# A relational step of TensorE in a graph network on one core: the sums first, then the edge weights, and one drain that carries the only signal

## What is computed

```python
edge_w = edge_attr @ nn_w.T + nn_b
msg = jax.nn.relu(x[src] * edge_w)
out = x @ root + bias
for r in range(N_REL):                      # 3 relations
    m = jnp.where((edge_type == r)[:, None], msg, 0.0)
    s = jax.ops.segment_sum(m, dst, num_segments=n)
    cnt = jax.ops.segment_sum(mask.astype(x.dtype), dst, num_segments=n)
    out = out + (s / jnp.maximum(cnt, 1.0)[:, None]) @ W[r]
```

## Time and profile before

| | |
|---|---|
| runs (us) | 5503.09, 5523.4, 5527.77; median 5523.4 |
| profiled execution (us) | 5528.27, span of its records 5526.4 |
| granted clock of TensorE, mean share of full | 0.81 |
| busy: PE, DVE, POOL, ACT | 68%, 52%, 49%, 27% |
| indirect DMAs of the relational gathers | 1248, 953 ns each on POOL |
| relational stretches, by layer (us) | 816, 765, 769 |

### The profile page before, as it was taken

One profiled execution on the slowest core, in us unless ns is written; L12 is line 12 of the kernel. 1 busy time (PEld: TensorE's weight loads), 2 busy tenths in 40 slices (PEclk: granted clock), 3 DMA queues, 4 the chain that ended last, 5 costly groups with the idle time before them and its releaser, 6 DMA issues. The chain is left out here.

```text
span 5526.4 us, 114815 instructions
## 1 busy us (share of the span) xinstructions
PE 3780.6 (68%) x28821; PEld 2930.4 (53%) x28821; DVE 2901.3 (52%) x10955; ACT 1517.5 (27%) x3933; POOL 2698.4 (49%) x2865
## 2 busy tenths in 40 slices
PE   4222175676666866676659888897777788777778
PEld 1111133444444344454438778786666677666667
DVE  6444454445455654444565555554555554555556
ACT  0000003555554155555522222211222221222220
POOL 4666603555555155555545455524555543555550
PEclk7555577978888998988867888898888889888888
DMA  1111126666666266666732222212322221222230
GB/s 40 23 23 23 22 89 193 174 173 170 173 174 141 89 175 173 176 171 174 172 104 80 76 80 79 82 49 81 85 80 83 82 66 59 82 82 81 84 85 30
DMA packets 375435, 563.79 MB, mean 102 GB/s; under 512 B 133583, under 2 KB 261632, under 8 KB 375362
## 3 DMA queue, kind: packets, MB, share of 16 engines
q0 software_dynamic: 155264, 442.19, 29.3%
q1 hardware_dynamic: 151576, 107.11, 6.9%
q10 hardware_dynamic: 68522, 13.62, 1.2%
HBM read 521.54 MB, written 41.08 MB: 102 GB/s over the span
## 5 line engine op out<-in xcount | busy, mean ns | idle before, releaser
L538 POOL DMA_INDIRECT gring<-h_rows,gidx x1248 | 1189.0, 953 | 1067.2 <-DVE rings L1646 723.8
L1067 PE MATMUL bank<-rings 128*128 128x96 f32 x6168 | 1047.0, 315 | 244.4 <-DVE region L1669 155.8
L1067 PEld LDWEIGHTS bank<-rings 128*128 128x128 f32 x6168 | 966.0, 226 | 348.7 <-DVE region L1669 217.7
L1052 PE MATMUL bank<-nnwt,rings 128*128 128x256 f32 x3084 | 993.6, 451 | 191.5 <-DMA rings<-edge_attr_T 136.9
L1646 DVE TENSOR_TENSOR rings<-bank,gring 128x256 f32<-128x256 f32 x1542 | 583.1, 420 | 954.0 <-remote 431.2
L1136 ACT ACTIVATE rings<-rings 128x512 f32<-128x512 f32 x771 | 485.6, 630 | 1853.1 <-DVE rings L1646 1540.0
L1052 PEld LDWEIGHTS bank<-nnwt,rings 128*128 128x128 f32 x3084 | 626.5, 225 | 271.4 <-DMA rings<-edge_attr_T 106.5
L1008 PE MATMUL bank<-rings 128*64 128x128 f32 x4096 | 399.2, 324 | 525.8 <-DVE ntop L1585 211.7
L506 POOL DMA_INDIRECT gring<-kv_rows,gidx x512 | 487.8, 953 | 457.7 <-PE bank L1034 202.9
L506 POOL DMA_INDIRECT ht<-kv_rows,gidx x512 | 491.9, 961 | 410.8 <-PE bank L1034 200.0
L1669 DVE TENSOR_TENSOR region<-region,bank 128x192 f32 x1542 | 540.0, 350 | 114.1 <-issue 15.8
(11 more groups left out here) (233 smaller groups left out, 4580.9 us busy)
## 6 DMA issues: line engine op xcount, KB each, us to landing
rings<-node_in_window_T SPq DMA_DIRECT2D x256, 128.0 KB
rings<-edge_attr_T SPq DMA_DIRECT2D x1548, 16.0 KB
gring<-h_rows,gidx POOLq DMA_INDIRECT x1248
kv_rows<-rows SPq DMA_DIRECT2D x50, 258.0 KB, 2.4
gring<-kv_rows,gidx POOLq DMA_INDIRECT x512
ht<-kv_rows,gidx POOLq DMA_INDIRECT x512
region<-edge_records SPq DMA_DIRECT2D x13, 576.0 KB, 5.9
edge_records<-rings POOLq DMA_INDIRECT x416
```

The source lines that it names most:

```text
L538: g.indirect_dma_start(out=gring_r[:, 2 * u + k, :], out_offset=None, in_=h_d[l], in_offset=bass.IndirectOffsetOnAxis(ap=gidx_r[:, half, 2 ...
L1052: ins = pe.matmul(bank[slot % RL][:, k * D:(k + 1) * D], eat[:, b, 2 * (slot % 2) + k, :], nnwt[:, :], start=True, stop=True)
L1067: ins = pe.matmul(b[:, (2 * k + c) * SEG:(2 * k + c + 1) * SEG], prod[:, slot % RL, (2 * k + c) * P:(2 * k + c + 1) * P], one, start=True, ...
```

## The change

On TensorE each step does the sums of pair p - 2 first, then the edge weights of pair p. No matmul carries a signal any more. Each step, also each of the two last ones that only sum, ends in `pe.drain()`, which raises the one semaphore `s_pe`. Per layer it counts 259 steps (`RPAIRS + LAG_SUM`). `s_ew` and `s_sp` are gone; who waited for them waits for `s_pe` with translated values: weights of pair p are step p, sums of pair p are step p + 2.

```diff
@@ SP
-                    wait_freed(sp, s_ew, l * RPAIRS + trip * U + u - 2)
+                    wait_freed(sp, s_pe, l * (RPAIRS + LAG_SUM) + trip * U + u - 2)
@@ relation_tiles, on TensorE
             def step(trip, u):
-                if live(trip, u, 0, RPAIRS):
-                    ...
-                    ins.then_inc(s_ew, 1)
                 if live(trip, u, LAG_SUM, RPAIRS):
                     ...
-                    ins.then_inc(s_sp, 1)
+                if live(trip, u, 0, RPAIRS):
+                    ...
+                    for k in range(2):
+                        ins = pe.matmul(bank[slot % RL][:, k * D:(k + 1) * D], eat[:, b, 2 * (slot % 2) + k, :], nnwt[:, :],
+                                        start=True, stop=True)
+                pe.drain().then_inc(s_pe, 1)
@@ related, on VectorE
+            done = l * (RPAIRS + LAG_SUM)
-                    v.wait_ge(s_ew, at + p + 1)
-                    wait_freed(v, s_sp, at + p - RL + 1)
+                    v.wait_ge(s_pe, done + p + 1)
+                    wait_freed(v, s_pe, done + p - RL + LAG_SUM + 1)
...
-                    wait_freed(v, s_sp, at + trip * U + u - 2)
+                    wait_freed(v, s_pe, done + trip * U + u - 2 + LAG_SUM)
...
-                    v.wait_ge(s_sp, at + p + 1)
+                    v.wait_ge(s_pe, done + p + 1 + LAG_SUM)
```

More of the change, by code:

```diff
@@ L402, in build @@
         s_eat = [sem(f"s_eat{i}") for i in range(2)]
-        s_oh, s_ew, s_prod, s_msg, s_sp, s_racc, s_rc = (sem(n) for n in ("s_oh", "s_ew", "s_prod", "s_msg", "s_sp", "s_racc", "s_rc"))
+        s_oh, s_pe, s_prod, s_msg, s_racc, s_rc = (sem(n) for n in ("s_oh", "s_pe", "s_prod", "s_msg", "s_racc", "s_rc"))
         s_clr = sem("s_clr")
@@ L1068, in step @@
                                             prod[:, slot % RL, (2 * k + c) * P:(2 * k + c + 1) * P], one, start=True, stop=True)
-                    ins.then_inc(s_sp, 1)
+                if live(trip, u, 0, RPAIRS):
+                    p, slot, r = tile_of(trip, u, 0)
+                    b = slot // 2 % 2
+                    if slot % 2 == 0:
+                        pe.wait_ge(s_eat[b], 16 * Q * (l * len(range(b, RQUADS, 2)) + r * (QUADS // 2) + slot // 4 + 1))
+                    wait_freed(pe, s_prod, at + p - RL + 1)
+                    for k in range(2):
+                        ins = pe.matmul(bank[slot % RL][:, k * D:(k + 1) * D], eat[:, b, 2 * (slot % 2) + k, :], nnwt[:, :],
+                                        start=True, stop=True)
+                pe.drain().then_inc(s_pe, 1)
             run_steps(pe, REXTRA + LAG_SUM, step, RTRIPS)
```

## The result

The changed kernel takes 5976.85 us (5975.99, 6007.05 and 5976.85), the kernel before 5523.4: 1.0853 times as long, 95% interval 1.0801 to 1.0906. The forecast was 5310 us, with a range up to 5660; the sign was wrong. The profiled execution has a span of 5974.0 us.

What follows compares the result with a forecast made beforehand. It took late TensorE signals, which make VectorE stand and POOL pause, to bound the relational loops. With the drain's signal on time, 0.28 us over 771 pairs saves 216 us: 5526 - 216 = 5310 us, range 5090 to 5660.

Steps and rivals of the forecast that it cites:

- The ring: Relational loops: late TensorE signal, VectorE stands, POOL finds no free slot and pauses, signal comes; 2.98 us a pair.
- Signals carried by matmuls arrive late: TensorE's signals to VectorE and SP: late by up to 18 us while POOL writes gathers; 431 us of VectorE's waits.
- rival A: TensorE's drain: its signal comes on time; 5310 us, from 5145 to 5490; chance 0.52.
- 216 us of gain: Relational loops: 2.70 us a pair against 2.98, 0.28 x 771, if the drain's signal is on time.
- Against C: Argument against late completions on TensorE: it works on in the stand, into other banks.
- C: TensorE: the completion under a matmul's signal is late, so the drain holds the engine; 5835 to 5980 us; chance 0.08.
- The drain's own price: TensorE's step: 0 to 0.5 us, 0.2 taken, giving 1.96 us, hidden under VectorE's 2.2.
- The order: TensorE's weights behind the relu wait: 1.3 us at each of 103 late wakes, up to 134 us; nothing if wakes vanish.
- SP: SP's slow issue of attribute loads in POOL's bursts: next late one, leaving 2.48 to 2.93 us a pair.
- D: Relational loops: lateness goes but SP's slow issue takes its place; 5490 to 5540 us; chance 0.15.
- The rule against it: TensorE's signals: increments serialize at some 26 ns each, so 771 fewer are worth 20 us and the drain a loss.

Runs made afterwards that it cites:

- e16_paced: Kernel before plus a POOL pause of some 0.4 us behind each two gathers, on a chip without late signals: 1.0030 of the kernel before.
- e18_by_layer: Changed kernel plus a signal-less drain ahead of the signalling one in layers 1 and 2, and POOL's pause in layer 2: 6071.2 us, 1.0846 of the kernel before.
- e11_order_no_gather: Kernel before with sums first, both signals on matmuls, no drain, and without gathers: 1.0071 of the kernel before with gathers (4307.2 us).
- e1_order: Kernel before with only the order changed, sums ahead of weights, both old signals on matmuls, no drain: 5733.4 us, 1.0223 of the kernel before.
- e2_one_matmul: Changed kernel with its one signal on the step's last matmul and no drain: 5750.4 us, 1.0269 of the kernel before.
- e3_plain_drain: Kernel before plus a signal-less drain at the end of each TensorE step, order and signals as before: 6324.1 us, 1.1273 of the kernel before.

## Why the prediction was wrong, point by point

- **The ring** (late signal, VectorE stands, POOL pauses) fits the kernel before: without gathers the waits that end "remote" are gone, and a layer takes 572 us for 765. Leaving out the gathers takes POOL's own time away too, but with all of them, on a chip without late completions, it is 580 us (e16_paced).
- **"Signals carried by matmuls arrive late"** is the step that failed. It is not the carrier but the completion beneath it: a drain without a signal is held too, 11.7 us behind its last matmul (e18_by_layer). The evidence offered, that VectorE's signals are prompt, speaks as well for TensorE's completions being late as for its signals, and rival A took it for the one. The 216 us of gain were therefore nothing, and VectorE's waits for TensorE grew from 737 to 1232 us.
- **Against C** stood that TensorE works on in the stand. It does, but the runs show that this tells nothing of a drain: matmuls start while signals are late, and a drain behind them stands. That argument excluded nothing, and C's 0.08 was too little. The Trainium skill's page "Perfetto Trace Analysis", section "Tensor Engine Instruction (MATMUL, LD_WEIGHTS)", cited there, has a matmul's update pushed once PSUM has acknowledged its bytes; e18_by_layer agrees, with a drain 11.7 us behind its matmuls and 13 ns for the signal behind it. C's time, 5835 to 5980, holds the result, but in part by luck: 103 held stands at 3 to 4.4 us, 309 to 453 us, were to carry it all. 100 drains are held over 1 us, 277 us in all, and about half of the loss was the drain's own price with the order's.
- **The drain's own price** was mis-sized: 0 to 0.5 us, 0.2 taken, 0.58 measured. The upper end names two parts, an overlap of 0.18 us and a first matmul of 0.45; added up they are 0.63, not 0.5. So it wasn't hidden: 2.34 us pass VectorE's 2.24.
- **Layer 0** was not looked at. The earlier trace rows has only layers 1 and 2. With the counts TensorE is the bound there once nothing is late (96% busy without gathers), and the drain's price was paid nearly in full: 140 of the 233 us, of which some 30 may be the order's (e11_order_no_gather).
- **The order**: 134 us with wakes as late as they were, 130 measured (e1_order). The size agrees, but in part by luck: "nothing if the wakes vanish" is 30 us (e11_order_no_gather), which that price left out, and no run shows the 1.3 us behind each wake by itself.
- **SP** as the next late one, the upper end of A and all of D, is refuted: its loads left out win 1.2%. And where nothing is late, layer 1 takes 580 us with all its loads (e16_paced, on another chip), 2.26 us a pair, less than the 2.48 to 2.93 that SP was to leave.
- **The rule against it**, in the Trainium skill's page "TensorE: Matmul & The Clock Gate", section "The cost: per-tile semaphore tail", says that a single increment on the last matmul is safe; that no drain is needed was my conclusion from it. The trace of this case agrees: with the signal on the last matmul (e2_one_matmul) the loss is 2.7% in place of 8.5%. Its 20 us for half the increments don't appear: e2_one_matmul takes 17 us more than e1_order, not less.

Together: the order 2.2%, the single signal 0.5%, the drain 5.7%, which multiply to the 8.5%, as they were taken one behind the other. In another sequence the shares differ: the drain alone in the old order is 12.7% (e3_plain_drain), and with the drain there the new order gains 1.7%, all of it in layer 0. By another cut: 4.1% (228 us of 5523) are there on both kinds of chip, and 4.4% come from the meeting with late completions: TensorE idles in the drain, returns at half clock and needs over 4 us a pair, and the order makes each late wake dearer. How much of that part is idle time and how much clock wasn't separated; the 277 us of held drains can't be set against it, since the kernel before lost time in the same stands.

## What to carry to other kernels

A drain on an engine that overlaps its groups costs that overlap and a gap in every step, here 0.58 us, and it turns each late completion from a latency that others may bridge into a stand of the engine. Put the signal on the last matmul; and before a cost is called hidden, look at the stage in which that engine has least slack, not only at the stages that look alike. If only one engine's signals are late, ask first whether the completion or the message is late: a drain with no signal ahead of the one with it tells.

## What the runs showed of the hardware

- The same kernel takes 5520 to 5604 us on some chips and 4277 to 4281 on others. In the relational layers the difference goes with TensorE's late completions: they come with gathers, and on some chips only. But over half of it, 660 of some 1240 us, lies ahead of these layers (the loops start at 2873 us in the kernel before, at 2212 in e16_paced), and nothing was tested there. Why these chips, and what in a gather holds a matmul's completion, stays open.
- The longest held drains stood 10.8 us (the changed kernel), 11.7 us (e18_by_layer) and 12.6 us (e3_plain_drain) behind the modelled end of their last matmul. Without a drain, TensorE started further matmuls while its signals were late.
- A drain cost 0.58 us of TensorE's step of 1.76 us. A second one behind it has a record of 13 ns and cost 0.08 us.
- With a drain behind the sums, TensorE stayed at the lower level of its clock (0.50) through a layer of 1200 us at 93 to 94% busy; with the drain behind the weights, the same layer had 0.78.
